# The second layer's routing search: constant steps, accumulating forms, fewer operations at both ends, and the next layer's weights split one batch earlier

## The reference, cut to what matters

```python
probs = softmax(xf @ gate_w.T)                       # 4096 tokens x 8 experts
order = argsort(-probs);  csum = cumsum(sorted probs)
k_idx = first place where csum >= 0.9                # experts up to there are assigned
R = p_sorted - rank  where assigned, else -1e9       # priority of a token at an expert
keep = the C = 4096/8 = 512 tokens with the largest R, per expert   # ties: lowest token first
scores_sel = where(assigned & keep, probs, 0)
h = gelu(x @ w1[e]);  y = sum_e scores_sel[:, e] * (h @ w2[e])

# attention of the same layer, per batch of 512 tokens, in 64 features
S = sigmoid(decay) * S + outer(v_t, k_t);  o_t = S @ q_t
```

## Time and profile before

| what | value |
|---|---|
| median of 3 runs | 1821.56 us (1819.24 to 1825.79) |
| the profiled execution | 1823.29 us, its span 1821.3 us |
| PE busy over the span | 1721.1 us, 94% |
| DVE, ACT, POOL busy | 1015.6, 831.5, 385.6 us |
| mean granted TensorE clock | 0.958 of full speed |
| the stage that is changed, after its normalisation | from about 454.1 to 564.8 us of the span |

### The profile page before, as it was taken

One profiled execution on the slowest core, in us unless ns is written; L12 is line 12 of the kernel. 1 busy time (PEld: TensorE's weight loads), 2 busy tenths in 40 slices (PEclk: granted clock), 3 DMA queues, 4 the chain that ended last, 5 costly groups with the idle time before them and its releaser, 6 DMA issues. The chain is left out here.

```text
span 1821.3 us, 22776 instructions
## 1 busy us (share of the span) xinstructions
PE 1721.1 (94%) x8614; PEld 1009.8 (55%) x8614; DVE 1015.6 (56%) x1662; ACT 831.5 (46%) x1022; POOL 385.6 (21%) x306
## 2 busy tenths in 40 slices
PE   7899999998888998999999999999999997999996
PEld 4232222324443445787878787787878673444443
DVE  4555555544874444544544545555445447888885
ACT  4667777774333334343433433433434325434432
POOL 1000000000662002112120302011121204655552
PEclk8699999998868999999999999999999998999998
DMA  1222222223004540000000000000000010000001
GB/s 76 50 47 47 47 47 48 47 47 121 1 1 118 149 106 1 1 1 1 1 1 1 1 1 1 1 1 1 1 1 2 1 42 16 1 1 1 0 1 46
DMA packets 19128, 49.12 MB, mean 27 GB/s; under 512 B 784, under 2 KB 1680, under 8 KB 18128
## 3 DMA queue, kind: packets, MB, share of 16 engines
q1 hardware_dynamic: 19024, 47.70, 10.9%
HBM read 45.21 MB, written 2.36 MB: 26 GB/s over the span
## 5 line engine op out<-in xcount | busy, mean ns | idle before, releaser
L498 ACT ACTIVATE probs<-ps_ring 128x1024 f32<-128x1024 f32 x256 | 245.9, 1024 | 89.8 <-PE ps_ring L735 86.8
L1797 PEld LDWEIGHTS ps_o<-v,probs 128*128 128x128 f32 x2048 | 235.3, 192 | 31.0 <-issue 25.3
L1797 PE MATMUL ps_o<-v,probs 128*128 128x129 f32 x2048 | 248.1, 278 | 1.7 <-ACT probs L1522 1.2
L1522 ACT ACTIVATE probs<-ps_ring 128x1024 f32<-128x1024 f32 x128 | 127.0, 1024 | 212.2 <-PE ps_ring L1778 212.1
L1603 DVE TENSOR_REDUCE negmax<-ps_o 128x2 f32<-128x1024 f32 x64 | 78.5, 1226 | 137.2 <-PE ps_o L1753 137.2
L749 PE MATMUL ps_o<-probs,v 128*32 128x512 f32 x1024 | 139.9, 621 | 0.7 <-DVE o_sb L559 0.6
L1515 ACT ACTIVATE xn<-ps_ring,pack 128x512 f32<-128x512 f32 x64 | 40.5, 685 | 162.7 <-PE ps_ring L1362 162.7
L1977 POOL TENSOR_TENSOR rs<-r,state 128x512 f32<-128x512 f32 x64 | 86.1, 1347 | 115.0 <-DVE state L2124 114.8
L1616 DVE RECIPROCAL rden<-ps_o 128x2 f32<-128x2 f32 x128 | 21.5, 168 | 144.2 <-PE ps_o L1797 144.2
L735 PEld LDWEIGHTS ps_ring<-q_stack,k_stack 32*128 32x128 f32 x512 | 32.0, 186 | 123.9 <-issue 101.7
L2124 DVE TENSOR_TENSOR_SCAN state<-decay,state,kv 128x511 f32<-128x511 f32 x64 | 91.4, 1428 | 6.9 <-issue 1.6
(11 more groups left out here) (380 smaller groups left out, 3447.2 us busy)
## 6 DMA issues: line engine op xcount, KB each, us to landing
cwb<-combine_by_expert SPq DMA_DIRECT2D x8, 2048.0 KB
score<-score_by_expert SPq DMA_DIRECT2D x7, 2048.0 KB, 13.7
pack<-pack_dram SPq DMA_DIRECT2D x1, 3840.0 KB, 15.6
pack<-pack_dram SPq DMA_DIRECT2D x1, 2507.0 KB, 8.6
x<-x_in SPq DMA_DIRECT2D x2, 1024.0 KB, 6.4
out<-x SPq DMA_DIRECT2D x1, 2048.0 KB, 6.3
score<-score_by_expert SPq DMA_DIRECT2D x1, 1536.0 KB, 13.6
pack<-pack_dram SPq DMA_DIRECT2D x1, 1451.0 KB, 6.7
```

The costliest lines, as they stand in the source:

```text
L498: nc.scalar.activation(probs[n % 3][:, 2 * half:2 * half + 2, :], ps, ACT.Exp, scale=float(HD0) ** -0.5).then_inc(read, 1)
L1522: nc.scalar.activation(probs[:, n % 2, m, :, :], ps, ACT.Exp).then_inc(read, 1)
L1797: last = nc.tensor.matmul(ps_o[:, i, k * (D + 1):(k + 1) * (D + 1)], probs[:, (b * PAIRS + p) % 2, m, j, queries], v[:, m, h, :], start=(m ...
```

## The change

- `ways` is now a row of 9 x 7 constants, the candidates' offsets of each search step (8/8^i times 1 to 7); the packed constants grow by 56 columns. `cand` is `ways_i + thr`, as a `tensor_scalar` that also accumulates into an unused column. `thr` is updated by a `tensor_scalar` with the step as a constant. The division of the step is gone.
- At the front, the reordered copy `prk` is issued before the second reduction, and six operations become four: `rank + 1 - pr` in one, `(mass < 0.9) * rank` in one, `(mass >= 0.9) * -1e9` in one, and a subtraction. The sign of `rank` is turned, so the result is the same up to rounding.
- At the end, `ge` and `eq` are multiplied by `prT` before the wait for `prefix`; after it stand a one-column operation (`last_tie`), one fused compare and multiply, and one addition, where there were four operations over 256 columns.
- The weights' split runs in iterations 3 to 7 instead of 4 to 8, in the same five pieces.

```diff
-        "ways": row(np.arange(1, 8)), ...
+        "ways": row(np.outer(8.0 / WAYS1 ** np.arange(1.0, STEPS1 + 1), np.arange(1, WAYS1)).reshape(-1)), ...
-FIRST_PIECE = 4
+FIRST_PIECE, PIECES = 3, 5
-            n = sh["w"][2].width // (B + 1 - FIRST_PIECE)
+            n = sh["w"][2].width // PIECES
-                if b >= FIRST_PIECE:            # ScalarE and GpSimd
+                if FIRST_PIECE <= b < FIRST_PIECE + PIECES:
             dve.drain()
+            nc.vector.tensor_copy(prk..., pr...)                  # moved up
+            dve.drain()
+            nc.vector.scalar_tensor_tensor(rank, rank, 1.0, pr, ALU.add, ALU.subtract)
             nc.vector.reduce_sum(mass, tie, AX_X)
             dve.drain()
-            nc.vector.tensor_scalar(mass, mass, 0.9, None, ALU.is_lt)
-            nc.vector.tensor_scalar(rank, rank, 1.0, None, ALU.add)
-            nc.vector.tensor_tensor(rank, pr, rank, ALU.subtract)
-            nc.vector.tensor_tensor(rank, rank, mass, ALU.mult)
-            nc.vector.tensor_scalar(mass, mass, 1.0, 1e9, ALU.subtract, ALU.mult)
-            nc.vector.tensor_tensor(rkk..., rank..., mass..., ALU.add)
-            nc.vector.tensor_copy(prk..., pr...)
+            nc.vector.scalar_tensor_tensor(rank, mass, 0.9, rank, ALU.is_lt, ALU.mult)
+            nc.vector.tensor_scalar(mass, mass, 0.9, -1e9, ALU.is_ge, ALU.mult)
+            nc.vector.tensor_tensor(rkk..., mass..., rank..., ALU.subtract)
             ...
-                nc.vector.tensor_scalar(cand[:, :], w["ways"], step, thr, ALU.mult, ALU.add)
+                step = 8.0 / WAYS1 ** (i + 1)
+                ways = w["ways"][:, i * (WAYS1 - 1):(i + 1) * (WAYS1 - 1)]
+                nc.vector.tensor_scalar(cand[:, :], ways, thr, None, ALU.add, ALU.add, accum_out=unused)
             ...
-                nc.vector.scalar_tensor_tensor(thr, moves, step, thr, ALU.mult, ALU.add)
-                dve.drain()
-                nc.vector.tensor_scalar(step, step, 1.0 / WAYS1, None, ALU.mult)
+                nc.vector.tensor_scalar(thr, moves, step, thr, ALU.mult, ALU.add)
             ...
+            nc.vector.tensor_tensor(ge[:, :], ge[:, :], prT[:, :], ALU.mult)
+            nc.vector.tensor_tensor(eq[:, :], eq[:, :], prT[:, :], ALU.mult)
             dve.wait_ge(prefix_done, 1)
-            nc.vector.tensor_scalar(cum, cum, ps[:, BANK_COUNT, 0:1], CAP + 0.5, ALU.add, ALU.is_lt)
-            nc.vector.tensor_tensor(cum, cum, eq, ALU.mult)
-            nc.vector.tensor_tensor(cum, cum, ge, ALU.add)
-            nc.vector.tensor_tensor(cum, cum, prT, ALU.mult).then_inc(scored, 1)
+            nc.vector.tensor_scalar(last_tie, ps[:, BANK_COUNT, 0:1], -1.0, CAP + 0.5, ALU.mult, ALU.add)
+            nc.vector.scalar_tensor_tensor(cum, cum, last_tie, eq, ALU.is_lt, ALU.mult)
+            nc.vector.tensor_tensor(cum, cum, ge, ALU.add).then_inc(scored, 1)
```

More of the change, by code:

```diff
@@ L116, in packed @@
     second = {
-        "ways": row(np.arange(1, 8)), "gate1": f["L1_ffn_gate_w"].T,
+        "ways": row(np.outer(8.0 / WAYS1 ** np.arange(1.0, STEPS1 + 1), np.arange(1, WAYS1)).reshape(-1)), "gate1": f["L1_ffn_gate_w"].T,
         "sum_expert": k["sum_expert"], "before_group": k["before_group"],
@@ L875, in layer1_route_and_attend @@
         ones = sb("n1_ones", [P, 2 * P])
-        s = sb("n1_small", [P, 4])
+        s = sb("n1_small", [P, 5])
         compared = first[:, :, :, :].rearrange("p t e f -> p (t e f)")
-        thr, step, moves, above = (s[:, i:i + 1] for i in range(4))
+        thr, moves, above, last_tie, unused = (s[:, i:i + 1] for i in range(5))
         cand, cnt, passed = (sb(f"n1_{n}", [P, WAYS1 - 1]) for n in ("cand", "count", "passed"))
@@ L1112, in _ @@
                     decay_o(b - 1)
-                if b >= FIRST_PIECE:
+                if FIRST_PIECE <= b < FIRST_PIECE + PIECES:
                     pool.wait_ge(high_ready, b - FIRST_PIECE + 1)
@@ L1153, in _ @@
             dve.drain()
+            nc.vector.scalar_tensor_tensor(rank[:, :, :], rank[:, :, :], 1.0, pr[:, :, :], ALU.add, ALU.subtract)
+            nc.vector.reduce_sum(mass[:, :, :], tie, AX_X)
+            dve.drain()
+            nc.vector.scalar_tensor_tensor(rank[:, :, :], mass[:, :, :], 0.9, rank[:, :, :], ALU.is_lt, ALU.mult)
+            nc.vector.tensor_scalar(mass[:, :, :], mass[:, :, :], 0.9, -1e9, ALU.is_ge, ALU.mult)
+            dve.drain()
+            nc.vector.tensor_tensor(rkk[:, :, :, :].rearrange("p k e g -> p g k e"),
+                                    mass[:, :, :].rearrange("p (g k) e -> p g k e", k=2),
+                                    rank[:, :, :].rearrange("p (g k) e -> p g k e", k=2), ALU.subtract)
+            dve.drain()
             nc.vector.memset(ones[:, :], 1.0).then_inc(ranked, 1)
             nc.vector.memset(thr, -8.0)
-            nc.vector.memset(step, 8.0 / WAYS1)
             dve.wait_ge(turned, 1)
@@ L1180, in _ @@
             nc.vector.tensor_tensor_scan(cum[:, :], ones[:, :], eq[:, :], 0.0, ALU.mult, ALU.add).then_inc(counted, 1)
+            nc.vector.tensor_tensor(ge[:, :], ge[:, :], prT[:, :], ALU.mult)
+            dve.drain()
+            nc.vector.tensor_tensor(eq[:, :], eq[:, :], prT[:, :], ALU.mult)
             dve.wait_ge(prefix_done, 1)
-            nc.vector.tensor_scalar(cum[:, :], cum[:, :], ps[:, BANK_COUNT, 0:1], CAP + 0.5, ALU.add, ALU.is_lt)
+            nc.vector.tensor_scalar(last_tie, ps[:, BANK_COUNT, 0:1], -1.0, CAP + 0.5, ALU.mult, ALU.add)
             dve.drain()
-            nc.vector.tensor_tensor(cum[:, :], cum[:, :], eq[:, :], ALU.mult)
+            nc.vector.scalar_tensor_tensor(cum[:, :], cum[:, :], last_tie, eq[:, :], ALU.is_lt, ALU.mult)
             dve.drain()
-            nc.vector.tensor_tensor(cum[:, :], cum[:, :], ge[:, :], ALU.add)
-            dve.drain()
-            nc.vector.tensor_tensor(cum[:, :], cum[:, :], prT[:, :], ALU.mult).then_inc(scored, 1)
+            nc.vector.tensor_tensor(cum[:, :], cum[:, :], ge[:, :], ALU.add).then_inc(scored, 1)
 def layer1_experts(nc, sh):
```

## The result

The changed kernel takes 1800.19 us (median of four runs, 1797.52 to 1801.06) against 1822.53 us (four runs, 1819.24 to 1825.79): a ratio of 0.9867, with a 95% interval from 0.9853 to 0.9881. That is 22.3 us less; the forecast was 1803.3. The profiled execution took 1797.52 us, 25.8 less than the one of before.

What follows compares the result with a forecast made beforehand. PE was taken to be held by DVE's late search operations and a lowered clock, with POOL's queue the next bound. POOL's floor -23.3 us plus 5 for the clock gave -18.3: 1803.3 by the median, range 1797 to 1815.

Steps and rivals of the forecast that it cites:

- the rival in which the update waits: Search: the new threshold update still waits for POOL, so only -13 us, 1808.5; chance 0.17.
- my strict reading: Threshold update: read strictly, the page's condition on the outermost dimension speaks against the plain one-column form; no size of its own.
- The terms of the sum: Whole stage: -23.3 us for POOL's floor with front and last piece, +5 for the clock, together -18.3.
- none over 0.5: Search's add-ups: PE has no wait over 0.5 us there, waiting at L952 for POOL's `later` instead.
- POOL's part: POOL's queue from batch 3: five iterations of 9.9 us, clearing `attended`, last `decay_o`; 52.9 us, stage ending at 541.0.
- +5 taken: PE late in the search: one fall of the clock after idling for `later` adds 5 us, bounds 0 and 14.
- The front: Before the search: five small operations instead of seven bring PE's `turn` 1.8 us earlier; at most 3.3, at worst 1.6 lost.
- worth nothing: Search's end: fewer operations behind `prefix` gain nothing, since the scores are stored 6.4 us before the stage ends.
- one hidden wait: Search's end: one new operation waits for `w_low`, as the 3.57 us one did; that wait was 3.1 us and hidden.
- more than 6: Search's end: `prefix` more than 6 us behind the last add-up would show the forecast wrong about the tail.
- my slower rival: Search's end: six operations wait for POOL, 9.8 us, delaying `prefix`; +6.6 us, 1828 if iterations gain nothing; chance 0.03.
- 3.4 us for it: Stage's end: moving the pieces removes the 3.42 us behind the last `decay_o`, whatever else happens; counted within the 52.9.

Runs made afterwards that it cites:

- the search alone: Kernel before with only the search's edits (constant steps, accumulating candidates, one-column threshold update, no division of the step); front, end, pieces unchanged: 1801.42 us, ratio 0.9883.
- the other two groups: Second and third groups of runs, each on its own chip; the changed kernel took 1801.79 us (0.9867) and 1801.19 us (0.9888) there against the kernel before.
- the tries here: Changed kernel with pieces in iterations 2 to 6: 1799.96 us; with accumulating `eq` written to PSUM: 1798.53 us; with both: 1802.81 us.
- the kernel with the pieces alone: Kernel before with only the weights' pieces moved to iterations 3 to 7 instead of 4 to 8: 1826.61 us, ratio 1.0016.
- the second group: Runs on another chip, where the changed kernel was timed again against the kernel before: 1801.79 us, ratio 0.9867.

## Why the prediction was right, point by point

**What bounds, and the rival forms: right.** The search's waits and the low clock behind them were most of the stage's 25 us; the search alone gives 1801.42. The update as a one-column `tensor_scalar` waits in none of nine cases, one of them begun at 493.31 inside the piece 491.27 to 494.76. So the rival in which the update waits is refuted. The condition in the Trainium skill, Vector Engine (DVE) Microarchitecture Reference, "5.1 Performance modes", is on the "most-non-unit-major dim", and one column has none: my strict reading asked of the page what it doesn't settle.

**The terms of the sum.** The update was mis-sized by 0.06 us (0.15 taken, 0.21 measured), the accumulating candidates 0.22 and 0.08 for the read (0.29 to 0.39 taken). An iteration of PE and DVE is 8.72 us; I had 8.8. One add-up waits 0.59 us, where I had said none over 0.5. POOL's part was to be 52.9 us from batch 3 on; it is 538.05 - 485.21 = 52.8. That it agrees so well is luck, a sum of two errors: I took 9.9 us a batch with gaps of 0.1, and it is 9.5 with nearly none, 2 us less in all; against that, the last batch takes 10.4 (its `later` is 3.52 us long and not 2.78), and the last `decay_o` waits 1.0.

**The clock: mis-sized, +5 taken, at most 1 measured.** It falls once, as I said, but behind `prefix`, not behind a wait for `later`; those waits are 0.3 and 0.8 us and do not bring it down. What follows the fall is one `states` (3.67 us), while POOL has a piece to do until 535.79, so only 1.01 us come out at `decay_o`. These are in the 52.8 already; with nothing added for the clock the sum gives 1821.6 - 23.3 = 1798.3 by the median, and measured is 1800.2. By the profiled executions the forecast of 1805.0 is 7.5 us too high: 5 of the clock, 1.5 of the front (next point) and 1.4 gained before `precedence`, less some 0.5 lost behind the stage. By the medians the miss is 3.1 us.

**The front: 1.8 taken, 2.3 and 1.1 measured.** From `precedence` to PE's `turn` it is 22.2 us before and 19.9 after in the profiles of these two kernels, and 1.1 us less in those in which `precedence` runs at its longer pace (below). At the shorter pace there is a part that I had not thought of. Before, PE waited 3.3 us for `ranked`, and the granted clock was 0.51 from 483 to 486, right behind it. Now it waits 1.0 and the clock stays at 1.00, so that POOL's batch 3 begins 26.1 us behind `precedence` and not 29.3: 3.3 us for 2.3. It can't be told from the time.

**The end: "worth nothing" came out, but for a reason I had not given.** I foresaw one hidden wait. There are two, 5.01 at `eq` and 4.76 at the last sum, and the first holds up `prefix` by 3.6 us. `prefix` comes 8.1 us behind the last add-up (519.83 to 527.95), and "more than 6" was my own sign of being wrong: the mechanism of my slower rival was there, at a third of its price. It didn't make the kernel slower because the search had gained 25 us and POOL's queue hid it: removing it moved the wait to `later` and did not shorten the stage.

**The waits' prices: wrong where I took them one by one.** I priced the update's wait at 5 us of the whole; put back alone it costs 0.7, within the noise, and the plain candidates alone 3 to 5. Together they cost 23. My account of the earlier trace rows explained each operation by what it met in POOL, and didn't ask what set *when* they met: the first wait. By the Trainium skill, SBUF — State Buffer, "Who interferes with whom", an instruction with two inputs in SBUF contends with GpSimd's reads and one with a single input outside the two-port modes doesn't. The trace agrees: the update with two inputs waits, the scan takes 1.59 us with both inputs in SBUF and 0.69 with one in PSUM. The second step, a release that lines the next instruction up, is from these runs alone.

**The pieces: mis-signed alone, and worth nothing in the sum.** With the old forms the move costs about 3 us, because a piece in batch 3 meets the candidates; my expectation for that run was 0 to 3.4 faster. In the changed kernel I took 3.4 us for it, within POOL's 52.9. The times don't show them: with move and front the ratio is 0.9867 to 0.9888, without both 0.9883. The profiles say why. Of the search alone there is one at the longer pace, and its stage is 84.0 us, against 85.8 of the changed kernel at the same pace. In the changed kernel `eq` begins 0.7 us ahead of a piece and loses all of it. Without the move POOL is some 2 us further on at that point: `eq` begins 1.2 us into the piece (527.18 against 526.00) and takes 2.43 us, PE waits 0.5 us at `prefix` and not 3.6, and the last `decay_o` waits for nobody, where it waits 2.93 us in the changed kernel. From the search alone, PE's wait and POOL's last piece:

```profile
PE n_ps L986 <- DVE score_rows L1179: 0.5, 1, 0.5
```

```profile
541.10 3.42 POOL L1116 TENSOR_TENSOR w_low<-pack,w_high 128x1536 fp32r<-128x1536 f32 x1
```

So what the last piece costs at the stage's end there, the search's end costs in the changed kernel. This rests on one profile of each.

Left open: the search with the new front and the pieces where they were was not run, so the move's share is not isolated. The search alone was timed on another chip than the other two groups, and 3 us are within their intervals.

## What to carry to other kernels

Where a short operation waits for another engine's long one, look at what released it: two small operations in a row that both wait can fall into step with the other engine and cost several times the sum of what they cost alone (23 us against 4 to 6 here), and taking one of them out of that step was nearly enough here. Before you value a removed stall, add up the queue of every other engine over the same stretch; the longest of them is the floor. Here 52.9 us were reckoned and 52.8 measured, in part by luck. A wait removed in front of a queue that bounds moved, in the tries here, to the next place that needed that queue.

## What the runs showed of the hardware

A plain DVE operation that begins during one of POOL's gapless instructions can lose the following ones too: `eq` took 5.01 us over `w_low` (3.49) and `kv` (0.72), the candidates of the kernel with the pieces alone 4.31 us over `decay_o` and `w_low`.

The front has two paces in executions of one and the same kernel. The 15 compares of `precedence` on DVE take 6.91 us in the profile of the changed kernel (start, duration, what) and 11.18 in its profile of the second group, on another chip:

```profile
459.15 6.91 DVE L300 TENSOR_TENSOR n_first<-n_prob 128x256 f32<-128x256 f32 x15
```

```profile
459.37 11.18 DVE L300 TENSOR_TENSOR n_first<-n_prob 128x256 f32<-128x256 f32 x15
```

The stage is then 85.8 and not 79.4 us, and the whole 1803.38 and not 1797.52. In seven of the fourteen profiles of this study it is the longer one. In all fourteen it goes with TensorE's clock: in the seven with the shorter pace the granted clock is still 0.50 in the four microseconds around the start of `precedence`, in the seven with the longer one it is 1.00. `within` of batch 0 and POOL's `kv` of batch 1 show it, in the changed kernel's first profile,

```profile
457.93 2.02 PE L943 MATMUL n_ps<-qv,k 64*128 64x128 f32 x8
```

```profile
466.92 0.73 POOL L1098 TENSOR_TENSOR kv<-kv,d_v 128x256 f32<-128x256 f32 x1 [2.85 <-ACT kv L1017]
```

and in the second:

```profile
457.53 1.11 PE L943 MATMUL n_ps<-qv,k 64*128 64x128 f32 x8
```

```profile
463.57 0.73 POOL L1098 TENSOR_TENSOR kv<-kv,d_v 128x256 f32<-128x256 f32 x1
```

With a faster TensorE, POOL has its next batch at once and doesn't pause for 2.85 us, and the compares, which have two inputs in SBUF, take longer beside it; PE then stands 7.1 us for `ranked` and not 1.0. That a faster engine slows the stage by 6.4 us in this way is my reading of fourteen profiles; no run changed the clock by itself. Profiles of two kernels should be compared from behind `precedence`, or with the same pace.
